# Attention and squared-ReLU block on 8 cores: bf16 stores of the first layernorm issued from SyncE instead of GpSimd, a rotated probability buffer, and four transpose buffers instead of two

## The reference

```python
x = x + tile(softmax(q k^T, axis=1) v, 16)         # q, k, v = LN(x) @ Wq, Wk, Wv;  D = 64
xn = LN(x); xp = xn shifted by one token
r = sigmoid((mu_r*xn + (1-mu_r)*xp) @ W_r^T)
k = square(relu((mu_k*xn + (1-mu_k)*xp) @ W_k^T))
x = x + r * (k @ W_v^T)                            # x: 4 x 4096 x 1024 f32
```

## Time and profile before

| | |
|---|---|
| time before, median of 2 runs | 720.64 us (720.12 to 721.16) |
| profiled execution | 723.02 us |
| its span, slowest core (core 4) | 721.5 us |
| spans of the 8 cores | 711.3 to 721.5 us |
| mean granted TensorE clock, by core | 0.721 to 0.737 |
| DMA moved by core 4 | 75.83 MB |

### The profile page before, as it was taken

How to read it: one execution, slowest core, us unless ns; L and a number is a source line. 1 busy time by engine, 2 the same in 40 slices (tenths; PEclk the granted TensorE clock), 3 DMA queues, 4 the chain that set the end, 5 groups by cost and what they waited for, 6 DMA issues and landing times.

```text
span 721.5 us, 5740 instructions; the slowest of 8 cores (711.3 to 721.5 us)
## 1 busy us (share of the span) xinstructions
PE 349.9 (48%) x1392; PEld 124.4 (17%) x1392; DVE 262.0 (36%) x483; ACT 294.5 (41%) x469; POOL 87.9 (12%) x93
## 2 busy tenths in 40 slices
PE   0004100004968777787773000000077999999993
PEld 0001000002421111111112000000022444444341
DVE  4702706237821111111122455422791002225665
ACT  4204004050019988898870166523673323330000
POOL 3201102011000030000000011000000000006884
PEclk9999655556985666666665555555577999999998
DMA  8945975845210079910000026365300000005885
GB/s 235 316 115 102 294 149 170 233 123 125 51 30 8 7 118 167 254 60 1 1 0 1 3 73 211 125 122 105 69 0 1 0 1 0 1 1 149 286 290 208
DMA packets 76997, 75.83 MB, mean 105 GB/s; under 512 B 59427, under 2 KB 59443, under 8 KB 76900
## 3 DMA queue, kind: packets, MB, share of 16 engines
q0 software_dynamic: 13504, 32.32, 17.4%
q1 hardware_dynamic: 21092, 32.62, 14.4%
q10 hardware_dynamic: 42368, 10.52, 8.7%
HBM read 47.79 MB, written 21.56 MB: 96 GB/s over the span
## 4 chain that ended last, share of the span: by engine, by line
PE 33%; DMA 20%; DVE 16%; issue 11%; ACT 10%; ACTq 7%; POOL 1%; DVEq 1%; SPq 0%; POOLq 0%
PE dpool L559 10%; PE ktp L965 8%; PE rps L925 7%; DMA zdram<-zst 6%; ACTq L377 5%; DMA y_out<-x2b 4%; ACT p_sb L624 4%; DMA z1T<-z1dram 4%; PE dpool L540 4%; DMA xst<-x_in 3%; DVE xk L904 3%; ACT zst L828 3%; DVE zst L418 2%; ACTq L847 2%; DVE sums L430 2%
## 5 line engine op out<-in xcount | busy, mean ns | idle before, releaser
L624 ACT ACTIVATE p_sb<-dpool,negm 128x1024 bf16<-128x1024 f32 x128 | 140.5, 1126 | 18.6 <-DVE ell L594 18.6
L925 PE MATMUL rps<-wrT,xr 128*128 128x512 bf16 x256 | 60.4, 402 | 144.8 <-DVE xr L897 136.2
L559 PE MATMUL dpool<-qrep,krep 64*128 64x512 bf16 x256 | 97.8, 547 | 42.2 <-ACT p_sb L624 34.1
L458 PE MATMUL qk<-zT,wqk 128*128 128x512 bf16 x64 | 18.5, 441 | 162.4 <-DVE qrep L489 97.7
L363 ACT ACTIVATE zst<-xst 128x1024 bf16<-128x1024 f32 x32 | 33.8, 1057 | 102.2 <-issue 92.7
L1022 PE MATMUL ops<-wvT,kaT 128*128 128x512 bf16 x256 | 56.4, 379 | 4.6 <-DVE tmp L1077 2.9
L925 PEld LDWEIGHTS rps<-wrT,xr 128*128 128x128 bf16 x256 | 26.1, 102 | 178.7 <-issue 151.7
L965 PE MATMUL ktp<-xk,wkT 128*128 128x512 bf16 x256 | 55.4, 379 | 1.3 <-ACT r_sb L938 1.3
L584 DVE TENSOR_REDUCE negm<-dpool 128x1 f32<-128x128 f32 x32 | 7.9, 287 | 126.3 <-PE dpool L559 126.3
L990 DVE TENSOR_TENSOR kaT<-kaT 128x512 bf16<-128x512 bf16 x32 | 13.6, 425 | 94.1 <-ACT kaT L981 94.0
L387 DVE TENSOR_SCALAR smean<-sums,cconst 128x4 f32<-128x4 f32 x12 | 2.8, 229 | 110.3 <-ACT zst L363 81.8
(11 more groups left out here) (85 smaller groups left out, 426.7 us busy)
## 6 DMA issues: line engine op xcount, KB each, us to landing
xst<-x_in SPq DMA_DIRECT2D x32, 512.0 KB, 10.0
xst<-x_in POOLq DMA_DIRECT2D x32, 512.0 KB, 6.2
zdram<-zst POOLq DMA_DIRECT2D x32, 256.0 KB, 9.5
y_out<-x2b SPq DMA_DIRECT2D x16, 512.0 KB, 4.5
z1dram<-z1b SPq DMA_DIRECT2D x16, 256.0 KB, 3.0
wrT<-wrT_in POOLq DMA_DIRECT2D x1, 2048.0 KB, 18.5
wkT<-wkT_in POOLq DMA_DIRECT2D x1, 2048.0 KB, 30.9
wvT<-wvT_in POOLq DMA_DIRECT2D x1, 2048.0 KB, 42.9
```

The lines of the kernel that those rows point to most:

```text
L458: t.matmul(qk[buf][:, :], wqk[:, ct * 128:(ct + 1) * 128], zT[ct][:, nch * 512:(nch + 1) * 512], start=(ct == 0), stop=(ct == CT - 1), ski ...
L559: t.matmul(units[u][:, cc * 512:(cc + 1) * 512], krep[64 * a:64 * (a + 1), kt * 128:(kt + 1) * 128], qrep[64 * a:64 * (a + 1), c * 512:(c ...
L624: sc.activation(p_sb[kt % 4][:, s * 1024:(s + 1) * 1024], units[u][:, :], AF.Exp, bias=negm[:, kt:kt + 1], accum_out=ellp[:, 4 * (kt % 4) + s:
L925: ins = t.matmul(r_ps[t_ % 3][:, hh * 512:(hh + 1) * 512], xr[ct][:, t_ * 128:(t_ + 1) * 128], wrT[:, ct * C + hh * 512:ct * C + (hh + 1) ...
```

## The change

Three edits.

1. The 32 stores to `zdram` are no longer issued by POOL. SP issues store i-8 directly behind load i, and the last eight stores at its end, each behind a wait for its apply.
2. Tile kt's exponentials go to `p_sb[(kt + 1) % 4]`. `p_sb0`, where `vT_sb` lies, is therefore first overwritten by tile 3, and the wait for the landing of its store moves from tile 0 to tile 3.
3. The transposes of stage E use four PSUM tensors instead of two, so PE waits for the copy of block b-4 instead of b-2.

```diff
--- before.py
+++ after.py
@@ -340,13 +340,14 @@
                     sy.wait_ge(SS, a_square(i - 8))
                 sy.dma_start(out=xst[:, s * C:(s + 1) * C],
                              in_=x_in[i * 128:(i + 1) * 128, :]).then_inc(DSs[s], 16)
-
-        @block.gpsimd
-        def _(g):
-            for j in range(TT):
-                g.wait_ge(SV, A_CNT[("apply", j)])
-                g.dma_start(out=zdram[j * 128:(j + 1) * 128, :],
-                            in_=zst[:, (j % 8) * C:(j % 8 + 1) * C]).then_inc(ZAs[j % 8], 16)
+                if i >= 8:
+                    j = i - 8
+                    sy.dma_start(out=zdram[j * 128:(j + 1) * 128, :],
+                                 in_=zst[:, (j % 8) * C:(j % 8 + 1) * C]).then_inc(ZAs[j % 8], 16)
+            for j in range(TT - 8, TT):
+                sy.wait_ge(SV, A_CNT[("apply", j)])
+                sy.dma_start(out=zdram[j * 128:(j + 1) * 128, :],
+                             in_=zst[:, (j % 8) * C:(j % 8 + 1) * C]).then_inc(ZAs[j % 8], 16)
 
@@ -540,7 +541,7 @@
-                                     p_sb[tt_ % 4][:, w * 512:(w + 1) * 512],
+                                     p_sb[(tt_ + 1) % 4][:, w * 512:(w + 1) * 512],
...
@@ -614,14 +615,14 @@
                         if s == 0:
-                            if kt == 0:
+                            if kt == 3:
                                 sc.wait_ge(SVT, 16)
...
-                        sc.activation(p_sb[kt % 4][:, s * 1024:(s + 1) * 1024],
+                        sc.activation(p_sb[(kt + 1) % 4][:, s * 1024:(s + 1) * 1024],
...
-        cm_tp = [nc.psum_tensor(f"tp{i}", [128, 64], F32) for i in range(2)]
+        cm_tp = [nc.psum_tensor(f"tp{i}", [128, 64], F32) for i in range(4)]
...
             for b in range(16):
-                if b >= 2:
-                    t.wait_ge(SV, e_tpev(b - 2))
+                if b >= 4:
+                    t.wait_ge(SV, e_tpev(b - 4))
                 hb = b // 8
-                t.transpose(tp_ps[b % 2][:, :],
+                t.transpose(tp_ps[b % 4][:, :],
```

More of the change, by code:

```diff
@@ L604, in _ @@
                     v.tensor_copy(xp_sb[:, kt:kt + 1],
-                                  p_sb[kt % 4][:, 4095:4096]).then_inc(SV, 1)
+                                  p_sb[(kt + 1) % 4][:, 4095:4096]).then_inc(SV, 1)
                 if q + 2 < KT // 2:
@@ L685, in _ @@
                 v.tensor_copy(out_tok[:, b * D:(b + 1) * D],
-                              tp_ps[b % 2][:, :]).then_inc(SV, 1)
+                              tp_ps[b % 4][:, :]).then_inc(SV, 1)
             v.wait_ge(SM, e_oxmm)
```

## The result

| | before | changed |
|---|---|---|
| median of the runs | 720.78 us (42 runs) | 717.45 us (43 runs) |
| profiled execution | 723.02 us | 718.14 us |
| span of the slowest core | 721.5 us | 716.5 us (core 1) |
| mean of the eight spans | 715.6 us | 709.5 us |

The ratio of the times is **0.9944, 95% interval 0.9925 to 0.9963**: 4.0 us faster, 2.7 to 5.4. Two later comparisons on other chips gave 0.993 and 0.9932. The time of 717.45 us lies in the range of 700 to 718, near its upper end; the forecast of a gain of 11.5 us was nearly three times what came. The medians are over all runs and the ratio over the undisturbed ones, so the ratio is what to read.

What follows compares the result with a forecast made beforehand. No engine was busy half the span, so waits between engines were taken as the bound. Terms -3.3 - 3.2 - 5.0 = -11.5 us from the profiled 723.0 gave 711.5; with the median 2.4 us lower, 709 us, range 700 to 718.

Steps and rivals of the forecast that it cites:

- Edit 2, -3.3 us: Start of stage D: ACT's exponential table load no longer waits for the store of vT_sb; 3.3 us sooner, bounds 2.5 to 3.4.
- Edit 3, -3.2 us: Stage E: sixteen block transposes take 3.4 us instead of 6.6 with four buffers; bounds -2.4 and -3.9 us.
- Edit 1, -5 us: Stage A: stores issued by SP instead of POOL let quarters 0 to 2 finish sooner; between -15.7 and +7.8 us.
- the terms -1, -2.5 and -1.5 us: Stage A: gains claimed from moving the stores to SP, for quarters 0, 1 and 2 in turn.
- the rate of 305 to 320 GB/s: Stage A: DMA rate claimed for quarters 1 (about 305) and 2 (320) with loads and stores in one queue.
- 222, 246 and 342 GB/s: Stage A, kernel before: 222 and 246 GB/s where only SP's loads flow, 342 where loads and stores both flow.
- the 18.4 and 18.5 of the prediction: Stage A: us that quarters 1 and 2 would take at 342 GB/s throughout, gains of 4.7 and 2.8 us.
- The bound of 8.2 us: Stage A, quarter 0: largest gain, if its 5.75 MB moved at 356 GB/s throughout, without the slow tail.
- the end of "unchanged": Stage A, quarter 0: -1 us taken, near the case where the DMA backlog moves with the stores and stays.
- The fourth quarter: Stage A's last stores, with no loads beside them: nothing won, 1 us of loss allowed inside the bounds.
- The first rival: Stage A: moving the stores to SP is worth nothing, quarters being bound by bytes; 714 us, chance 0.22.
- can move the slowest core by 3 us either way: After stage E: write of xrow_d, 12.01 us on core 4 and 6.21 on core 0, untouched by the change.

Runs made afterwards that it cites:

- quarter loads: Changed kernel with tiles 8 to 31 loading only 256 of 1024 columns, so work is left out; steps between quarters' transposes 38.1 and 37.1 us, stage A ends at 141.7.
- the late weights: Changed kernel with POOL's small weights issued only after the apply of tile 7; ratio to the kernel before 0.9899 (0.9847 to 0.9951).

## Why the prediction was right or wrong

**Edit 2, -3.3 us: right.** On the mean of the eight cores 5.8 - 2.6 = 3.2 us. ACT goes behind the first row maximum and no longer behind the store, and nothing of it is lost up to the last exponential.

**Edit 3, -3.2 us: right.** Measured 3.0 us; PE stands still only once, for 0.15 us, and a block takes 0.19 us.

**Edit 1, -5 us: wrong.** It was worth nothing: the terms -1, -2.5 and -1.5 us of quarters 0, 1 and 2 measured -0.6, +0.2 and +0.4 us (start of quarter 0's transposes, then the two steps, as means of the cores), which is none within the spread. The step that failed is the sentence "What can change is the rate. [...] With one queue that alternates, both kinds flow nearly all the time." and the rate of 305 to 320 GB/s that was made of it.

- The rate did not change: 6.3 MB took 23.0 and 22.1 us before and 23.1 and 22.2 us after. Both kinds did flow in one queue, and yet 342 GB/s was not held. Three of the windows of quarter 1 on core 4 of the changed kernel, its first, a middle one and its last:

```profile
68.00:71.00 3.00, 3.00 (x16) 1.36 (x14) 3.00 (x5) 2.60 (x5) 0.00 (x0) 1.00 0.65 171
...
77.00:80.00 3.00, 0.00 (x0) 0.00 (x0) 3.00 (x5) 0.00 (x0) 0.00 (x0) 0.50 1.04 263
...
89.00:91.20 2.20, 0.00 (x0) 0.00 (x0) 0.00 (x0) 0.00 (x0) 0.00 (x0) 0.50 0.26 102
```

  The six windows of 3 us from 71 to 89 us have 301, 303, 263, 352, 313 and 322 GB/s. So the 222, 246 and 342 GB/s of the earlier trace rows were moments of a few microseconds, read as rates of two mixes, and the prediction's rate had no room for a quarter's start and tail. What holds the middle near 309 GB/s at a share of about 1 was not found.
- The sum had no floor. The second burst comes 9.5 us behind the first whatever the DMA does. At full loads this takes little from the bound: at 342 GB/s the first 3.15 MB drain in 9.2 us, so a quarter could take 9.5 + 9.2 = 18.7 us instead of the 18.4 and 18.5 of the prediction. It decides where fewer bytes flow, as with quarter loads.

**Quarter 0.** The bound of 8.2 us rested on this: if the backlog "comes from the small weights, which POOL issued ahead of its stores, the stores now pass them". The weights were the cause, as the late weights show, and the stores did pass them in part. On core 4 those issued from 14 to 22 us (four from POOL, three from SP) land 26.8 and 9.9 us behind their issue (medians), the four issued from 24 to 34 us 19.6 and 13.5. But SP issues the last of them at 30.8 us, behind the loads, where POOL did at 28.7, and the tail stayed, at a share of 0.40. On the mean of the cores the transposes start 0.6 us sooner, and only a later issue of the weights brought 4.7 us. The choice near the end of "unchanged" was right for the time; the reason given for it, that the total per DMA engine does not change, is not what the late weights show: the same bytes issued later did take the tail away.

**The fourth quarter** was worth nothing, as said, although its stores did not lose but gain. Stores from SP land sooner (median 7.8 us for the 32 stores, 9.5 from POOL, on the slowest cores). Quarter 3's last four stores have no loads beside them, and from the moment when the first of them can be issued (0.9 us behind the start of its apply) to the transposes it takes 4.3 us instead of 5.7. So the last transposes start 1.5 us earlier on the mean (165.6, before 167.1). Yet nothing comes sooner by it. The chain of core 1 goes past these transposes:

```profile
162.07 1.53 DVE zst L419 x2
...
165.67 0.71 DVE qrep L490
...
166.51 3.31 PE qk L459 x8
```

From the last apply it goes over DVE's copies to PE, which then works for 22 us on blocks of q and k, the last ones those of quarter 3. The chain of the kernel before has the same steps. This is the one effect of edit 1 that every profile shows, and it lies beside the chain.

**The rule of the Trainium skill** that another issuing engine moves only the sequencer's time ("DMA: Bandwidth & Descriptors", "Issuing engines are not separate DMA queues") is what the time shows here: 1.0026 for edit 1 alone. The landings did change, as above. The rule of the Trainium skill on GpSimd's descriptors held up by VectorE ("SBUF — State Buffer", "Who interferes with whom") speaks for a gain that did not show in the time; no run here separates it.

**The sum.** The first rival's sum was 723.0 - 6.5 - 2.4 = 714 us, a gain of 6.5, and edits 2 and 3 measured 3.2 + 3.0 = 6.2 us. The mean span fell by 6.0 us in the profiles, and by 5.6 and 5.1 us (within 1.5) over the runs on two other chips; there the time of the slowest core fell by 4.8 us both times, and in the first comparison by 4.0. So little of the 6.2 us is missing on the mean, and the rest lies in which core is the slowest. The prediction had priced one scatter as what "can move the slowest core by 3 us either way", the write of xrow_d: 6.6 to 11.3 us by core in the changed kernel, 6.2 to 12.0 before. A second scatter had not been seen. From its first matmul to the end the last stage takes 65 to 79 us by core over all the profiles, with no edit near it and with a mean of 70.1 us both before and after. On core 1 of the changed kernel, the slowest, it takes 74.7 us, on core 4 of the kernel before 69.8. One of the waits in it, DVE's for the output's buffer, on core 1:

```profile
DVE tmp L1078 <- DMA y_out<-x2b: 20.4, 12, 2.6
```

and core 4 of the kernel before:

```profile
DVE tmp L1077 <- DMA y_out<-x2b: 12.4, 11, 2.2
```

So 4.9 us of the slowest core's span came back in a stage that the change does not touch. Whether this scatter explains all that is missing from 6.2 us was not shown.

## What to carry to other kernels

A rate read from a short window is not the rate of a stage: before pricing a transfer by bytes over a rate, take the rate from the first issue to the wait that ends, and find what releases the DMAs and how far apart the releases are. Where a burst drains before the next one comes, fewer bytes help the last burst alone; the cheap test is to load fewer bytes and see how much of the time goes. To make a store land sooner, take away what is queued ahead of it, and price what it then meets: here transposes beside loads. And where cores of one program differ by more than the change is worth, compare the mean of the cores over many runs before the slowest core of one profile.

## What the hardware showed that was not expected

- Eight DMA transposes of 128x1024 held ACT for 11 to 14 us alone, for 16 us beside four loads of 512 KB (mean of the cores; 14 to 18 by core), and for 23 to 26 us beside eight.
- Some 840 KB of small weights, issued before the first stores, were up to 40 us on their way, and the last of the stores of tiles 0 to 7 landed 5 us later for them (transposes from 45.2 us, 40.5 with the weights issued later). Stores from SP's queue landed 6 to 17 us sooner there than POOL's on core 4, and still the tail stayed.
- The write of one row of 64 numbers to DRAM, each from its own partition, took 6 to 14 us by core over all the profiles; in the changed kernel 6.6 to 7.3 us on cores 0, 2, 4 and 6 and 10.9 to 11.3 us on cores 1, 3, 5 and 7. What decides it was not looked into.
- The rate of one core's stores and loads was the same whether SP alone issued them or SP and POOL: 6.3 MB in 23.1 and 22.2 us, or in 23.0 and 22.1 (21 to 24 us by core).
- Four stores of 256 KB with no loads beside them let the transposes start 4.3 us after the first could be issued when SP issued them and 5.7 us after when POOL did, on every core of every profile in which quarter 3 has the order of the change or of the kernel before.
